# A convolution by minimal filtering: two outputs per four products, or four outputs per six

## The chip, the cores and the metric

The program runs on one core of a Trainium2 chip. Time is the device time of one launch in microseconds (us), from three runs; the profile is of one execution. The engines are named as the profile names them: PE (TensorE, matrix products; PEld its weight loads), DVE (VectorE), ACT (ScalarE), POOL (GpSimd) and SP (SyncE, which here only issues DMAs). Each engine runs its own list of instructions in order, and semaphores hold it where it needs another's result.

## The reference

Two blocks follow each other on x, of 2 batches x 1024 positions x 1024 channels, float32:

```
x = x + attention(layernorm(x))
    conv: 3 taps along the positions, 1024 -> 768 channels, padding 'SAME', + bias
    split into q, k, v of 256; 16 heads of 64, in blocks of 128 positions
    causal softmax(q k / 8) v; output 1024 -> 256, projection 256 -> 1024
x = x + lora_dense(layernorm(x))
    x W^T + b, plus four small expert products weighted by a softmax router
```

All is float32. The change is in the convolution: y[t] = w0 x[t-1] + w1 x[t] + w2 x[t+1], where each w is a 1024 x 768 matrix, and in the order in which positions lie in memory behind it.

## The kernel before, in words

**Stages.** The layer norm of a batch goes tile by tile (128 positions): DVE makes statistics, POOL the power, ACT or DVE scales, PE transposes eight 128x128 pieces, and ACT copies them from PSUM to `xT`, where channels lie on partitions. Then comes the convolution, then attention in steps of two heads and 256 positions, then the dense part in 16 tiles of 128 positions.

**The products.** The convolution takes pairs of positions. For every pair, each of the 8 chunks of 128 input channels and each of 6 chunks of 128 output channels, four products are summed over chunks in four PSUM banks: of differences and sums of four neighbouring inputs (`u`, by DVE in `transform`) with w0, w2, and (w0 + w2 +- w1)/2 (made by POOL's three additions in `mix`; the half comes at the evacuation). A "step" is one chunk of output channels of one batch, 12 in all; it has 512 pairs, so each product has 512 columns, and there are 8 chunks x 4 = 32 products in a step.

**Native and split.** Three steps multiply float32 as it is (`native_unit`). The other nine use `three_pass`: both operands are split in a high part, rounded by ACT to the short type fp32r (`high_weight`, `high_input`), and a low part, the rest, by DVE (`low_weight`, `low_input`), and PE runs high x high, high x low and low x high:

```
    pe.matmul(out, w_hi, x_hi, start=first, stop=False)
    pe.matmul(out, w_hi, x_lo, start=False, stop=False)
    return pe.matmul(out, w_lo, x_hi, start=False, stop=last)
```

**Order.** It is written out by hand. `ORDER` lists 48 slots (k) of two input chunks each; tables (`U_AT`, `HIGH_AT`, `LOW_AT`, `TURN_AT`, `STATS_AT`) say in which slot each engine does what for the second batch beside the products of the first. Raw weights are loaded by SP in a ring of `RR` = 3, split weights lie in a ring of `WR` = 2: the high part for slot k + 1 waits until PE has left slot k - 1. At the end of a step ACT evacuates one bank with the bias and DVE adds the others (`outputs`), and SP stores the result `cy` in DRAM (`c_scratch`), from where attention loads it by groups of 256 positions (`c_raw`); ACT and POOL split it again (`c_hi`, `c_lo`).

**Hand-over to attention.** The load of group 0 is issued in slot 31 and that of group 1 in slot NK - 2. Queries and keys of attention steps 0 and 1 are computed inside the last two slots of the convolution. The last step's outputs are made by DVE behind attention step 2, for `HEAD` = 3.

## Time and profile before

| | us |
|---|---|
| three runs | 915.65, 916.17, 920.49 |
| median | 916.17 |
| span of the profiled execution, first to last instruction | 915.3 |
| PE busy | 873.6 |
| DVE, ACT, POOL busy | 439.7, 395.7, 326.3 |

The profiled execution's own time on the device isn't listed apart from the three runs; its span lies 0.9 us under their median and 0.4 us under the lowest, which is what lies around a span. Matmuls are pipelined and their ends are modelled: their starts tell the pace. A wait is listed under the engine that ended it.

### The profile page before, as it was taken

The page shows a single profiled execution, that of the slowest core. Times are in us where ns is not written, and L with a number is a line of the kernel's source. Part 1 is how long each engine was busy: PE and PEld are TensorE (multiplying, and loading weights), DVE is VectorE, ACT ScalarE, POOL GpSimd, SP SyncE. Part 2 cuts the span into 40 slices and gives each one's busy share as a digit, 9 for nine tenths or more (in the row PEclk, how much of TensorE's full clock was granted, in tenths as well). Part 3 has the DMA queues.
Part 4 walks back from the last instruction along what each step waited for, and adds up shares of the span by engine and source line. Part 5 has one row for each costly group of instructions (what it writes and reads, how often), then busy time and mean ns, then how long its engine had stood idle before and what let it go on. Part 6 is the DMA issues. An engine that isn't in the chain of part 4 may idle for free.

```text
span 915.3 us, 14506 instructions
## 1 busy us (share of the span) xinstructions
PE 873.6 (95%) x5376; PEld 726.6 (79%) x5376; DVE 439.7 (48%) x1238; ACT 395.7 (43%) x1024; POOL 326.3 (36%) x295
## 2 busy tenths in 40 slices
PE   3799999998999979999999999999988999999997
PEld 3345788846888868888888888888867999999997
DVE  6944774958453333433323332433267444444442
ACT  5601332741332256867676767676674111111110
POOL 3454756548665222433343424342223100000000
PEclk9899999999999999999999999999999999999999
DMA  6145333225433332012125232020312312221211
GB/s 235 41 137 182 94 92 95 74 72 187 131 104 94 121 116 105 1 35 93 35 93 218 94 88 98 31 93 1 139 61 79 116 52 87 93 92 50 90 47 47
DMA packets 41291, 85.01 MB, mean 93 GB/s; under 512 B 9091, under 2 KB 27523, under 8 KB 40580
## 3 DMA queue, kind: packets, MB, share of 16 engines
q1 hardware_dynamic: 38916, 75.69, 25.2%
q0 software_dynamic: 2304, 8.39, 2.2%
q8 instruction: 43, 0.70, 0.3%
q14 instruction: 28, 0.23, 0.1%
HBM read 60.60 MB, written 23.07 MB: 91 GB/s over the span
## 4 chain that ended last, share of the span: by engine, by line
PE 88%; DVE 5%; ACT 2%; issue 2%; DMA 1%; POOL 1%; DVEq 0%; ACTq 0%
PE net_psum L62 20%; PE net_psum L63 19%; PE net_psum L64 19%; PE net_psum L913 8%; PE net_psum L997 4%; PE net_psum L1036 4%; PE net_psum L1004 4%; PE net_psum L1051 3%; PE net_psum L1052 2%; PE net_psum L1053 2%; PE net_psum L1065 2%; PE net_psum L895 1%; DVE x_lo L661 1%; PE net_psum L1121 1%; PE net_psum L906 1%
## 5 line engine op out<-in xcount | busy, mean ns | idle before, releaser
L405 POOL TENSOR_TENSOR pr<-pr,rrec 128x512 f32<-128x512 f32 x64 | 66.6, 1041 | 244.7 <-DVE rrec L708 244.7
L62 PE MATMUL net_psum<-fw_hi,xT_hi 128*128 128x354 f32 (+1 forms) x384 | 126.5, 329 | 0.0
L64 PE MATMUL net_psum<-fw_hi,xT_lo 128*128 128x354 f32 (+1 forms) x384 | 124.9, 325 | 0.0
L63 PE MATMUL net_psum<-fw_lo,xT_hi 128*128 128x354 f32 (+1 forms) x384 | 124.8, 325 | 0.0
L62 PE MATMUL net_psum<-x_hi,w_hi 128*128 128x512 f32 x288 | 114.3, 397 | 4.1 <-DVE w_lo L666 4.1
L63 PE MATMUL net_psum<-x_lo,w_hi 128*128 128x512 f32 x288 | 112.8, 392 | 0.0
L64 PE MATMUL net_psum<-x_hi,w_lo 128*128 128x512 f32 x288 | 112.7, 391 | 0.0
L715 DVE CUSTOM_DVE_ANT_0 pr<-net_psum,mask 128x128 f32<-128x128 f32 x256 | 58.8, 286 | 103.3 <-PE net_psum L997 103.3
L522 ACT ACTIVATE pr<-pr,negmax 128x128 f32<-128x128 f32 x256 | 99.0, 390 | 12.5 <-DVE negmax L715 12.5
L473 ACT ACTIVATE w_hi<-raw 128x1024 fp32r<-128x1024 f32 x36 | 38.1, 1058 | 134.9 <-PE net_psum L64 88.8
L385 POOL TENSOR_TENSOR raw<-raw 128x256 f32<-128x256 f32 x48 | 56.5, 1177 | 95.8 <-DMA raw<-in_conv_w 95.8
L913 PE MATMUL net_psum<-u,raw 128*128 128x512 f32 x192 | 85.6, 608 | 4.8 <-DVE u L650 4.8
L666 DVE TENSOR_TENSOR w_lo<-raw,w_hi 128x1024 fp32r<-128x1024 f32 x36 | 50.5, 1402 | 80.2 <-ACT w_hi L473 80.1
L62 PE MATMUL net_psum<-c_hi,wqk_hi 128*128 128x256 f32 x256 | 78.6, 307 | 2.6 <-ACT kf L529 2.6
L913 PEld LDWEIGHTS net_psum<-u,raw 128*128 128x128 f32 x192 | 37.3, 195 | 51.3 <-issue 50.7
L64 PE MATMUL net_psum<-c_hi,wqk_lo 128*128 128x256 f32 x256 | 73.3, 286 | 0.0
L63 PE MATMUL net_psum<-c_lo,wqk_hi 128*128 128x256 f32 x256 | 73.2, 286 | 0.0
L63 PEld LDWEIGHTS net_psum<-fw_lo,xT_hi 128*128 128x128 f32 x384 | 72.9, 190 | 0.0
L64 PEld LDWEIGHTS net_psum<-fw_hi,xT_lo 128*128 128x128 f32 x384 | 72.9, 190 | 0.0
L62 PEld LDWEIGHTS net_psum<-fw_hi,xT_hi 128*128 128x128 f32 x384 | 72.7, 189 | 0.0
L62 PEld LDWEIGHTS net_psum<-x_hi,w_hi 128*128 128x128 f32 x288 | 54.4, 189 | 16.9 <-DVE w_lo L666 5.2
L438 POOL DMA_DIRECT2D out<-y x16 | 9.4, 585 | 156.3 <-DVE y L804 156.3
(137 smaller groups left out, 1892.6 us busy)
## 6 DMA issues: line engine op xcount, KB each, us to landing
raw<-in_conv_w SPq DMA_DIRECT2D x48, 384.0 KB, 3.7
xn<-in_x SPq DMA_DIRECT2D x16, 512.0 KB, 5.0
xr<-in_x SPq DMA_DIRECT2D x8, 1024.0 KB, 4.9
x_scratch<-xr SPq DMA_DIRECT2D x8, 1024.0 KB, 4.0
x1t<-x_scratch SPq DMA_DIRECT2D x16, 512.0 KB, 4.1
out<-y POOLq DMA_DIRECT2D x16, 512.0 KB, 5.0
c_scratch<-cy SPq DMA_DIRECT2D x12, 512.0 KB, 3.3
c_raw<-c_scratch SPq DMA_DIRECT2D x8, 768.0 KB, 4.8
```

The source lines that it names most:

```text
L62: pe.matmul(out, w_hi, x_hi, start=first, stop=False)
L63: pe.matmul(out, w_hi, x_lo, start=False, stop=False)
L64: return pe.matmul(out, w_lo, x_hi, start=False, stop=last)
L385: pool.tensor_tensor(r[:, :, 3], r[:, :, 1], r[:, :, 2], ALU.add).then_inc(s["sum_ready"], 1)
L405: pool.tensor_tensor(pr[:, jj % 4], pr[:, jj % 4], rrec[:, jj % 4].unsqueeze(2).to_broadcast([P, UN, P]), ALU.mult).then_inc(s["p_ready"], 1)
L473: act.activation(w_hi[:, r % WR], raw[:, k % RR, :, 1:5], ACT.Copy).then_inc(s["w_hi_ready"], 1)
L522: e = act.activation(pr[:, jj % 4, un], pr[:, jj % 4, un], ACT.Exp, bias=negmax[:, jj % 2, un:un + 1], scale=-1.0, accum_out=rsum[:, jj % ...
L666: dve.tensor_tensor(w_lo[:, r % WR], raw[:, k % RR, :, 1:5], w_hi[:, r % WR], ALU.subtract).then_inc(s["w_lo_ready"], 1)
L715: m = dve.tensor_tensor_reduce(out=pr[:, jj % 4, un], in0=scp[:, h, b * P:(b + 1) * P], in1=mask[:], scale=-DH ** -0.5, scalar=-MASKED, op ...
L913: mm = pe.matmul(acc[st % 2][:, v, :], raw[:, k % RR, c % 2, 1 + v], u[:, c, v], start=c == 0, stop=c == DC - 1)
L997: mm = pe.matmul(scp[:, h, t], qf[e, jj % 2, t], kf[e, jj % 2, t], start=True, stop=True)
L1004: mm = pe.transpose(ptp[:, un * P:(un + 1) * P], pr[:, jj % 4, un], ident[:])
```

## The change

The pairs become quads: four outputs from six products. Every point has 256 quads a batch (`QUADS`), 512 over both (`QT`).

- Two of the six products, those with the raw taps w0 and w2, are native float32, `first_unit`, for all 6 output chunks: 24 units `a`, each two input chunks x two output chunks x two points, of 256 columns, one batch after the other. Their inputs `ua` are made by DVE (`first_inputs`), two operations of 512 elements for a chunk of a batch. ACT takes the sums to `stage`, SP stores them in DRAM (`m_scratch`) and loads them again for the outputs.
- The other four products are split passes of 512 columns over both batches, `split_unit`: 24 units `k`, each two input chunks of one output chunk. Their inputs `u` take DVE six operations per chunk and batch (`inputs_of`, 256 to 512 elements) or seven to eight for both batches (`inputs`), then one high part and one low part of 2048 elements per chunk. Their weights are taps scaled by ACT (`pre_scale`), one sum of 512 elements by POOL and two by DVE (`mix`).
- Both batches are normalised and transposed before the split units; the second one's transposes stand behind units 4 to 7. The evacuation writes four planes of positions apart (`stepped`), so all tokens lie within a tile in the order residue by residue of 4. Loads of x, stores of the result and the causal mask follow that order: each such DMA becomes two of 64 rows (four where it had two tiles), the mask four operations.
- The outputs take two ACT operations and ten of DVE in three groups (`halves`, `sums`, `ends`) per output chunk of both batches, where a step of one batch took one and four.
- Attention steps 0 and 1 stand behind the convolution. The loads of group 0 and of the attention biases are issued in slot NK - 2, behind the store of the fifth output; output chunk 5 of group 0 is taken from SBUF. The load of group 1 stands behind the store of the last output.

The core of the diff:

```diff
+    DUOS = MC // 2
+    NP4 = DC // 2
+    NA = N * DUOS * NP4
+    NK = MC * NP4
+    AW, RR, WR, ST = 4, 3, 2, 4
...
             def conv_slot(k):
-                if k in LOAD_AT:
...
+                if k == NK - 2:
+                    sync.wait_ge(s["unit_done"], k)
+                    sync.dma_start(wv_raw[:], wv).then_inc(s["wv_loaded"], 16)
+                    sync.wait_ge(s["c_stored"], 16 * LAST)
+                    sync.dma_start(c_raw[:, 0:LAST], c_dram[0:LAST, :, 0:GT].rearrange("m p l -> p m l")).then_inc(s["early_loaded"], 16)
                     for dst, src in ((bqk_c[:, 0], bq), (bqk_c[:, 1], bk), (bv_c[:], bv), (bo_c[:], bo)):
                         sync.dma_start(dst, src).then_inc(s["early_loaded"], 16)
...
-                    sync.wait_ge(s["c0_lo_ready"], 1)
-                    load_c(1)
...
+            load_c(1)
...
-                pool.wait_ge(raw_loaded[k % RR], 16 * (k // RR + 1))
-                pool.tensor_tensor(r[:, :, 3], r[:, :, 1], r[:, :, 2], ALU.add).then_inc(s["sum_ready"], 1)
-                pool.wait_ge(s["sum_ready"], k + 1)
-                pool.tensor_tensor(r[:, :, 4], r[:, :, 3], r[:, :, 0], ALU.subtract)
-                pool.tensor_tensor(r[:, :, 3], r[:, :, 3], r[:, :, 0], ALU.add).then_inc(s["mix_ready"], 1)
+                pool.wait_ge(s["pre_ready"], k + 1)
+                pool.tensor_tensor(r[:, :, 3:5], r[:, :, 1:3], r[:, :, 3:5], ALU.add).then_inc(s["ef_ready"], 1)
 
...
+            def pre_scale(k):
+                r = raw[:, k % RR]
+                act.wait_ge(raw_loaded[k % RR], 32 * (k // RR + 1))
+                act.activation(r[:, :, 2], r[:, :, 1], ACT.Copy, scale=0.5)
+                act.activation(r[:, :, 4], r[:, :, 3], ACT.Copy, scale=2.0).then_inc(s["pre_ready"], 1)
...
+            def first_inputs(n, c):
+
+                cols = slice(n * QUADS, (n + 1) * QUADS)
+                for i in range(c, c + 2):
+                    dve.scalar_tensor_tensor(ua[:, i, :, cols], pair(i, n, P2, P1), -5.0, pair(i, n, P0 + 1, P3), ALU.mult, ALU.add).then_inc(s["ua_part"], 1)
+                for i in range(c, c + 2):
+                    dve.wait_ge(s["ua_part"], DC * n + i + 1)
+                    dve.scalar_tensor_tensor(ua[:, i, :, cols], pair(i, n, P0, P3 - 1), 4.0, ua[:, i, :, cols], ALU.mult, ALU.add).then_inc(s["ua_ready"], 1)
...
+            def mix(k):
+
+                r = raw[:, k % RR]
+                tap = r[:, :, 0:1].to_broadcast([P, 2, 2, P])
+                dve.wait_ge(s["ef_ready"], k + 1)
+                dve.tensor_tensor(r[:, :, 1:3], r[:, :, 3:5], tap, ALU.add)
+                dve.tensor_tensor(r[:, :, 3:5], r[:, :, 3:5], tap, ALU.subtract).then_inc(s["mix_ready"], 1)
...
+                a, o = acc[m % 2], cy[m]
+                b2, b4 = (a[:, v].rearrange("p (b i) -> p b i", i=32) for v in (M2, M4))
+                dve.wait_ge(s["t_ready"], 2 * m + 1)
+                dve.scalar_tensor_tensor(o[:, :, O0], b2, C_A, o[:, :, O1], ALU.mult, ALU.add)
+                dve.scalar_tensor_tensor(o[:, :, O1], b2, -C_A, o[:, :, O1], ALU.mult, ALU.add)
+                dve.wait_ge(s["t_ready"], 2 * m + 2)
+                dve.scalar_tensor_tensor(o[:, :, O2], b4, C_B, o[:, :, O3], ALU.mult, ALU.add)
+                dve.scalar_tensor_tensor(o[:, :, O3], b4, -C_B, o[:, :, O3], ALU.mult, ALU.add).then_inc(s["halved"], 1)
+
...
+                o = cy[m][:, lo:hi]
+                m5, m0 = (ma[m][:, v].rearrange("p (b i) -> p b i", i=32)[:, lo:hi] for v in range(2))
+                dve.wait_ge(s["halved"], m + 1)
+                dve.wait_ge(s["ma_loaded"], 16 * (m + 1))
+                dve.scalar_tensor_tensor(m0, m0, 0.25, o[:, :, O2], ALU.mult, ALU.add)
+                dve.tensor_tensor(m5, m5, o[:, :, O1], ALU.add)
+                dve.scalar_tensor_tensor(o[:, :, O2], o[:, :, O2], 4.0, o[:, :, O0], ALU.mult, ALU.add)
+                return dve.scalar_tensor_tensor(o[:, :, O1], o[:, :, O3], 2.0, o[:, :, O1], ALU.mult, ALU.add)
...
+                m5, m0 = (ma[m][:, v].rearrange("p (b i) -> p b i", i=32)[:, lo:hi] for v in range(2))
+                dve.tensor_tensor(o[:, :, O0], o[:, :, O0], m0, ALU.add)
+                return dve.scalar_tensor_tensor(o[:, :, O3], o[:, :, O3], 8.0, m5, ALU.mult, ALU.add)
...
-                        dve.tensor_tensor(wqk_lo[:, i], wqk_raw[:, i], wqk_hi[:, i], ALU.subtract).then_inc(s["qk_w_lo_ready"], 1)
+                if k == 0:
+                    low_input(DC - 1)
+                if k + 2 < NK:
+                    mix(k + 2)
+                if m >= 0 and k % NP4 == 0:
+                    halves(m)
+                if m >= 0 and k % NP4 == 1:
+                    sums(m, 0, TOK // P).then_inc(s["add_step"], 1)
+                    dve.wait_ge(s["add_step"], m + 1)
+                    ends(m, 0, TOK // P).then_inc(s["cy_ready"], 1)
...
+            for c in range(0, DC, 2):
+                first_inputs(1, c)
+            for c in range(DC):
+                if c == DC - 2:
+                    mix(0)
+                    mix(1)
+                inputs(c)
+                if c:
+                    low_input(c - 1)
+                if c == DC - 2:
+                    low_weight(0)
+            for k in range(NK):
                 conv_slot(k)
...
+            sums(LAST, 0, GB).then_inc(s["add_done"], 1)
+            dve.wait_ge(s["add_done"], 1)
+            ends(LAST, 0, GB).then_inc(s["head_ready"], 1)
+            dve.wait_ge(s["c5_hi_ready"], 1)
...
+            sums(LAST, GB, TOK // P).then_inc(s["add_done"], 1)
+            dve.wait_ge(s["add_done"], 2)
+            ends(LAST, GB, TOK // P).then_inc(s["cy_ready"], 1)
...
+            def first_unit(a):
+
+                n, p, d = a // (DUOS * NP4), a % NP4, a // NP4
...
+                for c in range(2 * p, 2 * p + 2):
+                    pe.wait_ge(s["ua_ready"], DC * n + c + 1)
+                    for mi in range(2):
+                        for v in range(2):
+                            mm = pe.matmul(duo_acc(d, mi)[:, v * QUADS:(v + 1) * QUADS], wa[:, a % AW, mi, c % 2, 1 - v],
+                                           ua[:, c, v, n * QUADS:(n + 1) * QUADS], start=c == 0 and v == 0, stop=c == DC - 1,
+                                           skip_group_check=True)
+                mm.then_inc(s["a_done"], 1)
...
+            def split_unit(k):
+
+                m, p = k // NP4, k % NP4
+                pe.wait_ge(s["w_lo_ready"], k + 1)
+                if p == 0:
...
+                for c in range(2 * p, 2 * p + 2):
+                    if m == 0:
+                        pe.wait_ge(s["x_lo_ready"], c + 1)
+                    for v in range(NV):
+                        mm = three_pass(pe, acc[m % 2][:, v, :], w_hi[:, k % WR, c % 2, v], w_lo[:, k % WR, c % 2, v],
+                                        x_hi[:, c, v], x_lo[:, c, v], c == 0, c == DC - 1)
                 mm.then_inc(s["unit_done"], 1)
-
...
+            for a in range(NA):
+                first_unit(a)
+                for j in TURN_AT.get(a, ()):
+                    transpose_tile(1, j)
             for k in range(NK):
-                conv_slot(k)
...
```

## Rows read from the trace of the kernel before

**Rows 1.** the page, busy time by engine; chain that ended last.
```profile
PE 873.6 (95%) x5376; PEld 726.6 (79%) x5376; DVE 439.7 (48%) x1238; ACT 395.7 (43%) x1024; POOL 326.3 (36%) x295
...
PE 88%; DVE 5%; ACT 2%; issue 2%; DMA 1%; POOL 1%; DVEq 0%; ACTq 0%
```

**Rows 2.** windows: stretch; length, busy (count) by engine, PE clock, DMA share, GB/s.
```profile
28.77:86.06 57.29, 57.29 (x129) 25.25 (x129) 35.88 (x32) 16.97 (x10) 24.84 (x21) 0.95 0.37 122
...
86.06:203.00 116.94, 115.36 (x498) 87.86 (x497) 83.21 (x111) 47.03 (x41) 69.98 (x68) 1.00 0.30 92
...
230.00:326.60 96.60, 96.60 (x438) 80.08 (x436) 40.70 (x37) 27.81 (x29) 47.83 (x47) 1.00 0.40 128
...
350.00:700.00 350.00, 345.37 (x2725) 287.51 (x2725) 133.75 (x675) 241.30 (x798) 124.05 (x90) 0.99 0.23 80
```

**Rows 3.** PE's waits: waiting line, releaser, us in total, times, longest.
```profile
PE net_psum L913 <- DVE u L650: 4.8, 1, 4.8
...
PE net_psum L62 <- DVE w_lo L666: 4.1, 2, 2.6
```

**Rows 4.** timeline of PE, three stretches: start us, us, engine, line, operation.
```profile
84.31 0.19 PEld L913 LDWEIGHTS net_psum<-u,raw 128*128 128x128 f32 x1 [0.24 <-issue]
...
84.74 0.19 PEld L913 LDWEIGHTS net_psum<-u,raw 128*128 128x128 f32 x1 [0.24 <-issue]
...
90.58 0.39 PE L62 MATMUL net_psum<-x_hi,w_hi 128*128 128x512 f32 x1
...
91.26 0.39 PE L62 MATMUL net_psum<-x_hi,w_hi 128*128 128x512 f32 x1
...
322.51 0.28 PE L63 MATMUL net_psum<-c_lo,wqk_hi 128*128 128x256 f32 x1
...
322.63 0.28 PE L64 MATMUL net_psum<-c_hi,wqk_lo 128*128 128x256 f32 x1
```

**Rows 5.** chain of waits: eight transposes in a row; start us, us, what.
```profile
721.28 0.87 PE net_psum L1065 x8
```

**Rows 6.** timeline, DVE and POOL: start us, us, engine, line, operation, tiles.
```profile
25.14 1.23 DVE L648 TENSOR_TENSOR u<-xT 128x1024 f32<-128x1024 f32 x1 [2.72 <-ACT xT L455]
...
172.06 1.23 DVE L650 TENSOR_TENSOR u<-xT 128x512 f32<-128x512 f32 x1
...
178.46 0.68 DVE L649 TENSOR_TENSOR u<-xT 128x512 f32<-128x512 f32 x1
...
179.06 0.68 DVE L650 TENSOR_TENSOR u<-xT 128x512 f32<-128x512 f32 x1
...
208.50 2.67 POOL L387 TENSOR_TENSOR raw<-raw 128x256 f32<-128x256 f32 x1
```

**Rows 7.** windows, near the start.
```profile
30.00:32.00 2.00, 2.00 (x3) 0.77 (x3) 2.00 (x4) 0.57 (x1) 0.89 (x1) 0.50 0.00 0
```

**Rows 8.** groups by form: line, operation, tiles, count | busy, mean ns | idle.
```profile
L666 DVE TENSOR_TENSOR w_lo<-raw,w_hi 128x1024 fp32r<-128x1024 f32 x36 | 50.5, 1402 | 80.2 <-ACT w_hi L473 80.1
...
L661 DVE TENSOR_TENSOR x_lo<-u,x_hi 128x2048 fp32r<-128x2048 f32 x16 | 40.3, 2551 | 12.2 <-PE net_psum L913 12.2
...
L473 ACT ACTIVATE w_hi<-raw 128x1024 fp32r<-128x1024 f32 x36 | 38.1, 1058 | 134.9 <-PE net_psum L64 88.8 <-POOL raw L388 46.2
...
L405 POOL TENSOR_TENSOR pr<-pr,rrec 128x512 f32<-128x512 f32 x64 | 66.6, 1041 | 244.7 <-DVE rrec L708 244.7
```

**Rows 9.** DMA issues: tiles, queue, count, KB each, median us to landing.
```profile
c_scratch<-cy SPq DMA_DIRECT2D x12, 512.0 KB, 3.3
...
c_raw<-c_scratch SPq DMA_DIRECT2D x8, 768.0 KB, 4.8
```

**Rows 10.** timeline at the start of attention, ACT and PE.
```profile
337.91 0.83 ACT L533 ACTIVATE c_hi<-c_raw 128x768 fp32r<-128x768 f32 x1
...
343.18 0.66 PE L1004 MATMUL net_psum<-ident,pr 128*128 128x128 f32 x4
```

**Rows 11.** tile raw: one group's duration in ns, min/median/max.
```profile
L387 POOL TENSOR_TENSOR raw<-raw x48: 724/742/7260, 21.9 to 305.2; 128x256 f32<-128x256 f32 x48
```

More of the change, by code:

```diff
@@ L109, in act_scaled @@
     def act_scaled(n, j):
-        return (LT - len(DVE_SCALES)) * n + sum(i not in DVE_SCALES for i in range(j + 1))
-    def splits(k):
-        return 0 <= k < NK and not native[k]
+        return LT + j + 1 - len(DVE_SCALES) if n else sum(i not in DVE_SCALES for i in range(j + 1))
     NG = TOK // GT
@@ L247, in network, with turned, duo_acc, pair @@
         block = ctx.enter_context(nc.Block())
-        def turned(n, i):
-            if n == 0:
-                return acc[i % 4 // 2][:, 2 * (i % 2):2 * (i % 2) + 2, :]
-            return acc[0 if i < 6 else 1][:, 2 * (i % 2):2 * (i % 2) + 2, :]
+        def turned(n, j):
+            i = 2 * (j % 4) if n == 0 else 2 * (j % 2)
+            return psum[:, i:i + 2]
+        def duo_acc(d, mi):
+            return psum[:, 4 + 2 * (d % 2) + mi]
+        def pair(c, n, first, second):
+            row = (N * c + n) * ROW
+            return stepped(xT, row + first, (second - first, 2), (1, QUADS))
+        def both(c, first, second):
+            return stepped(xT, N * c * ROW + first, (second - first, 2), (ROW, N), (1, QUADS))
         def is_step(jj):
@@ L437, in store @@
                 pool.wait_ge(s["y_ready"], NB * (t + 1))
-                pool.dma_start(out[t * P:(t + 1) * P], y[:, t % 2]).then_inc(y_stored[t % 2], 16)
+                for half in range(2):
+                    pool.dma_start(rows_by_quads(out[t * P:(t + 1) * P], half), y[64 * half:64 * half + 64, t % 2]).then_inc(y_stored[t % 2], 16)
             for t in range(TT):
@@ new lines, in first_out, with high_input @@
+            def first_out(d):
+                act.wait_ge(s["a_done"], NP4 * (d + 1))
+                for mi in range(2):
+                    i = 2 * d + mi
+                    wait(act, a_stored[i % ST], 16 * (i // ST))
+                    act.activation(stage[:, i % ST].rearrange("p v i -> p (v i)"), duo_acc(d, mi), ACT.Copy).then_inc(s["a_evac"], 1)
+            def high_input(c):
+                act.wait_ge(s["u_ready"], c + 1)
+                act.activation(x_hi[:, c], u[:, c], ACT.Copy).then_inc(s["x_hi_ready"], 1)
@@ L497, in conv_slot @@
-                if k == QK_AT:
+                if k == 0:
+                    high_input(DC - 1)
+                if k % NP4 == 0 and k:
+                    evacuate(k // NP4 - 1)
+                if k + 2 < NK:
+                    pre_scale(k + 2)
+                if k in (10, 14):
+                    i = (k - 10) // 4
                     act.wait_ge(s["qk_w_loaded"], 16 * 2)
-                    for i in range(2):
-                        act.activation(wqk_hi[:, i], wqk_raw[:, i], ACT.Copy).then_inc(s["qk_w_hi_ready"], 1)
```

521 lines of the change are left out of this document (279 added, 242 removed).

## The prediction

> **What bounds the kernel now.** First the page's busy times and the chain of work that ended last: PE is busy 873.6 of 915.3 us and holds 88% of the chain; DVE and ACT are under half busy [rows 1]. The reader is to see there that only PE time is worth anything. Second the stages: PE is full in the native stage (28.77 to 86.06), in the split stages and in attention, at full clock but for short stretches [rows 2]. Third PE's waits: in the whole convolution it waits 4.8 us at the start for the first DVE inputs and 4.1 us for low weights [rows 3]. So the convolution, 28.8 to 326.6 us, is as long as its matmul columns. Fourth PE's pace: three split passes of 512 columns start every 0.68 us, 0.2267 us each; a native 512-column matmul leaves two records, each with its weight load, 0.43 us apart; a 256-column pass starts every 0.12 us [rows 4].
>
> **PE work removed and added.** Before: 9 of 12 steps are split, 9 x 32 x 3 = 864 passes; after: 6 x 8 x 4 x 3 = 576. 288 x 0.2267 = 65.3 us go. Native before: 96 matmuls of 512 columns, 192 records. After: 6 x 8 x 2 points x 2 batches = 192 matmuls of 256 columns, 384 records. Low end: half of 0.43, 0.215 each, 82.4 us, as now. High end: 256 columns cost 0.12/0.2267 = 0.53 of 512 in split passes, so 0.228, 87.4 us. I take 0.217, 83.3 us, near the low end, since the fixed part of a native record is small. The 64 transposes of the second batch stay, 0.109 us each by my estimate from eight of them in 0.87 us [rows 5], 7.0 us.
>
> **First stage, on the clock of the trace.** DVE begins its inputs at 25.1 as now [rows 6]; twice as many x DMAs of half the rows could move this by 0 to 0.5 us, taken as 0. It needs three 512-element operations and one wait for its own result before PE can start. Clean operations of 512 start 0.60 apart [rows 6], so PE starts at 25.1 + 1.9 = 27.0 against 28.77. Later inputs come at 2.5 us a pair of chunks against 3.47 us of PE, hidden. PE's clock is 0.50 in the window from 30 us [rows 7], and that costs 2.7 us of work today; I keep it (0 to 4). ACT scales and evacuates the second batch inside units 4 to 7, about 18 us of ACT in 24; hidden. DMA: 0.5 MB per 3.47 us is 151 GB/s; the same stage now moves 122 GB/s at a share of 0.37 [rows 2], so some 330 is to be had. PE ends the stage at 27.0 + 83.3 + 7.0 + 2.7 = 120.0.
>
> **Hand-off to the split stage, where I expect DVE late.** Transposes end at 27.0 + 2.7 + 8 x 3.47 + 7.0 = 64.5, their evacuation at 66. From there DVE runs without a gap: inputs of the second batch, 16 x 0.60 + 0.4 = 10; then, by 0.07 + n/960 us per operation of n elements (which gives 0.60 for 512), a second-half input of chunks 0 to 3 is 2.8, of chunks 4 to 7, both batches, 5.05; a low input is 2.2 when POOL is still (the mean with POOL beside it is 2.55 [rows 8]). Up to the first low weight: 10 + 4 x 2.8 + 3 x 5.05 + 6 x 2.2 + 5.5 (two mixes, 1.3 each, and about 3 us behind ACT's pre-scale, which stands behind two evacuations, and POOL) + 1.2 = 56.3, done at 122.3. PE waits 2.3. Before the second low weight stand one input 5.1, a low input 2.2, and itself 1.2 (1.4 in the mean today [rows 8]): 130.8; PE was due at 127.7 and waits 3.1. The third stands behind the last low input, POOL's sum, the mix, ACT's high weight: 2.2 + 2.3 + 1.1 + 1.3 = 137.7 against 136.2, 1.5. In all 6.9 us, and 1.3 for half clock after such a gap. Behind a late low weight stands only PE; all of it is on the path. Bounds: 0, if DVE finds 10 us that I double-counted, to 16, if each of some 75 operations costs its full 0.68 rather than its 0.60 step and each wait more.
>
> Here the Trainium skill would charge more. The steps of 0.60 under durations of 0.68 [rows 6] show overlap of neighbours. The page VectorE: DVE Perf Modes, section The DRAIN you can't avoid, says that after every operation the next doesn't start until the pipe is empty; by that every operation costs its whole duration, and the sum would be 75 x 0.08 = 6 us longer (867). The row speaks against it for operations with no wait between them.
>
> **Split stage.** 24 units of 24 passes, 24 x 5.44 = 130.6 us. Per unit DVE has a mix (2 x 0.60) and a low weight (1.15); per four units also 10 operations of 512 for the outputs, 6.2: 4 x 2.4 + 6.2 + 1 of waits = 16.8 of 21.8 us. The order is tighter than the sum: high weight 1.06 (ACT), pre-scale 0.7 (two of 256, from that), POOL's sum 1.04 by its 128x512 row [rows 8], mix 1.2 and 0.4 of semaphores make a loop of 4.4 us per unit against 5.44, with evacuation 5.7 in one of four. The low weight behind the six sums then comes about 0.8 us before PE wants it. A POOL operation that meets a DVE one on SBUF adds about 0.55 to it (1.23 instead of 0.68) [rows 6]; twice that for 512 elements. So between 0 and 2 us at each of five seams; I take 0.5, 2.5 in all. PE's split work ends at T = 120.0 + 6.9 + 1.3 + 130.6 + 2.5 = 261.3. Check: 326.6 less 2.9 (queries and keys of two steps that lie inside the convolution now), less 65.3, plus 0.9 native, less 1.8 start, less 5.5 old waits and their slow clock, plus 10.7 new ones is 262.7.
>
> **Start of attention.** Two head steps that lay under the last units now come after T, and two loads are late. (1) Outputs 0 to 4 are in DRAM only after DVE's fifth outputs at T - 7: store 3.3, load of c_raw with four bias loads 4.8 [rows 9] and issues: T + 1.5; ACT's high part 1.3, DVE's low part 1.4: T + 4.3, and only then queries and keys of step 0. (2) DVE goes on: halves 2.5, sums of two blocks 1.2, waits for ACT's copy and PE's second step until 10.0, first maxima 0.9, sums of fourteen blocks 3.4: T + 14.4. Store 3.3, load 4.8: c_raw of group 1 at T + 22.7. ACT's step 3 waits for it; today the load is issued before the convolution ends and ACT splits it at 337.91, 11.3 after [rows 10]. Behind this wait on ACT stand its copy 0.8, the transposed probabilities 0.6, the exponentials 1.5, q and k 0.9; PE's step 5 waits for the last: T + 26.4. Today PE starts those queries just after the four transposes of 343.18 [rows 10], at 343.9, 17.3 after. One more us for half clock: 27.4 - 17.3 = 10.1 us given back. Bounds: 3 (both loads hidden, only the 2.9 of PE work) to 14. From there attention is PE-bound at full clock [rows 2] and its code is the same; more, smaller loads and stores of x and out are hidden, with 0.5 (0 to 1) at the last store.
>
> **Sum.** 915.3 - (326.6 - 261.3) + 10.1 + 0.5 = 860.6. The profiled span lies 0.9 under the median of 916.17 (915.65 to 920.49), so I forecast 861.5.
>
> **Rivals.** A: as above, 861.5, own range 854 to 869; chance 0.50.
> B: DVE keeps up and the two loads are hidden in PE's backlog. 861.5 less 10.7 and 5 is 846. For it: DVE is only 48% busy [rows 1]. Against it: the queue in DVE after 66 us is counted from rows and leaves no gap. 0.16.
> C: DVE is later than I think: 6 us more in the hand-off, 1.5 more at each of five seams, 2 of clock: 877. For it: POOL's 256-element operation took 0.74 in the median and up to 7.3 [rows 11]. Against it: POOL has no work while most of the inputs are made. 0.29.
> D, slower than before: the serial loop of the weights takes the place of PE. If each POOL sum waits out a DVE operation (2.7, as L387 takes beside a low input [rows 6], and 0.6 for its greater length) and each mix is doubled by it (2.4), the loop is 1.06 + 0.7 + 3.3 + 2.4 + 0.4 = 7.9 us per unit, 24 x (7.9 - 5.44) - 2.5 = 56.5 more: 918. From 7.7 us a unit on nothing is left of the gain. Against it: in this order DVE mostly waits for POOL's sum, so only the low weight is beside it. 0.04. That the split passes weren't cut can't be: the count follows from the loops. That the 256-column native records cost as much as 512 ones (943) is excluded by the 0.12 against 0.2267; 0.01 with what I forgot, inside no change.
>
> The page SBUF — State Buffer, section Who interferes with whom, says that a DVE instruction with two SBUF inputs and a GpSimd one that reads SBUF shut each other out for a whole instruction. It is the rule by which D would come about; the rows agree (1.23 against 0.68 [rows 6]), but only where both have work at once.
>
> **Numbers.** A, B, C are faster: 0.95; same 0.01; slower 0.04. About 0.5% (4.6 us) is what a measurement of this kernel can tell from no change. From 847 to 880 holds B's end, A, and most of C.
>
> **What would show it.** 576 split passes, and 384 native records near 0.217 apart. PE's first native matmul near 27, its first split one near 122, waits for low weights or x_lo of about 7 us in the first three units, and little at the seams. PE's last split pass near 261. DVE without a gap from 66 to 130. ACT's first c_hi of group 1 waiting for a DMA some 5 us, about 23 us after the last pass. A mean POOL sum over 2 us or a pace of units well over 5.44 would show C or D; no PE waits around 120 would show B. The forecast is wrong in kind if attention's pace of later steps changes at all.

## The result and the profile after

The changed kernel takes 1092.05 us, median of 4 runs (1088.8 to 1093.62), against 916.0 us of the kernel before on the same chip: a ratio of 1.190, 95% interval [1.186, 1.194]. It is 19% slower where 861.5 (847 to 880) and "faster" had been forecast. Sign and size are both wrong.

The page of the kernel after, for [rows 1]: busy time, and the chain that ended last (the profiled span is 1087.0 us).

```profile
PE 835.5 (77%) x5280; PEld 727.1 (67%) x5280; DVE 451.7 (42%) x1337; ACT 390.8 (36%) x1068; POOL 209.3 (19%) x194
...
PE 47%; SPq 15%; issue 10%; DVE 10%; DMA 8%; POOL 5%; ACT 4%; DVEq 0%; POOLq 0%; ACTq 0%
...
L63 PE MATMUL net_psum<-x_hi,w_hi 128*128 128x512 f32 x192 | 77.5, 404 | 6.7 <-DVE w_lo L804 6.5
...
xn<-in_x SPq DMA_DIRECT2D x32, 256.0 KB
xr<-in_x SPq DMA_DIRECT2D x32, 256.0 KB
```

PE does less work, as forecast: 3 x 192 = 576 split passes, 835.5 us busy against 873.6. But it holds 47% of the chain and not 88%. SP's queue, nowhere in the chain before, holds 15%, DMA 8%. What waits, in the groups of waits (line, releaser, us in total, times, longest), first PE, then DVE, then POOL:

```profile
PE net_psum L1092 <- DMA wa<-in_conv_w: 64.4, 1, 64.4
PE net_psum L1173 <- POOL pr L463: 50.5, 6, 10.7
PE net_psum L1077 <- ACT xn L510: 46.0, 3, 29.0
...
PE net_psum L63 <- DVE w_lo L804: 6.5, 5, 3.0
...
DVE cstats L734 <- DMA xn<-in_x: 132.4, 15, 13.6
...
POOL xr L472 <- DMA xr<-in_x: 133.7, 7, 28.9
```

All three large PE waits lead back to a load of x. In the first stage DVE waits for the x tiles themselves; the native weights wa stand in SP's queue behind the x tiles of the second batch and come 64.4 us late; in attention, POOL waits for xr, the rows of x to be added, and its normalizations of probabilities, for which PE waits, stand behind that. Against the few us of waits of [rows 3] this is another kernel. What the loads do, by SP's part of the timeline, by tile xn (duration in ns, min/median/max) and by windows (length, busy by engine, PE clock, DMA share, GB/s):

```profile
27.47 34.90 SPq L290 DMA_DIRECT2D xn<-in_x  x6
...
L290 SPq DMA_DIRECT2D xn<-in_x x32: 504/4848/10297, 2.0 to 152.1; - x32
...
20.00:40.00 20.00, 2.88 (x12) 2.48 (x13) 3.43 (x10) 3.40 (x3) 1.10 (x2) 1.00 0.13 52
203.48:244.96 41.48, 41.48 (x193) 36.51 (x193) 39.60 (x59) 13.51 (x14) 0.00 (x0) 1.00 0.65 199
580.00:600.00 20.00, 12.30 (x84) 10.36 (x84) 3.99 (x22) 7.84 (x27) 8.43 (x5) 0.74 0.21 70
```

The DMA engines are busy at a share of 0.13, two of sixteen, and move 52 GB/s; nothing else is under way. In the median, one DMA of 256 KB keeps SP for 4.85 us before the next can be issued. The kernel before loads the same x from 4 to 10 us at a share of 1.01 and 402 GB/s:

```profile
4.00:10.00 6.00, 0.00 (x0) 0.00 (x0) 4.15 (x11) 0.82 (x1) 1.12 (x2) 1.00 1.01 402
```

The second of the changed kernel's three windows is a native stretch without transposes: 192 records (193 in the window) in 41.46 us, 0.216 each, for a forecast of 0.217. The third is attention at a place where xr is late: PE 12.3 of 20 us busy, and the clock at 0.74, a mean between its two levels, behind the idle time.

### The profile page after: what moved, and what is told of

The parts are those of the page before. It is cut to its first block, busy times and chain, and to the rows that moved or that the text cites. A ratio compares the mean times of both kernels' runs of the same rounds, so it can differ in the third digit from the quotient of the medians.

```text
span 1087.0 us, 14438 instructions
## 1 busy us (share of the span) xinstructions
PE 835.5 (77%) x5280; PEld 727.1 (67%) x5280; DVE 451.7 (42%) x1337; ACT 390.8 (36%) x1068; POOL 209.3 (19%) x194
## 4 chain that ended last, share of the span: by engine, by line
PE 47%; SPq 15%; issue 10%; DVE 10%; DMA 8%; POOL 5%; ACT 4%; DVEq 0%; POOLq 0%; ACTq 0%
SPq L290 12%; PE net_psum L63 10%; PE net_psum L64 9%; PE net_psum L65 9%; PE net_psum L1092 5%; DMA xr<-in_x 4%; PE net_psum L1173 3%; SPq L296 2%; PE net_psum L1166 2%; PE net_psum L1205 2%; POOL raw L446 2%; DVE raw L797 2%; POOL xr L472 2%; PE net_psum L1220 1%; DMA wa<-in_conv_w 1%
## 5 line engine op out<-in xcount | busy, mean ns | idle before, releaser
L1092 PE MATMUL net_psum<-ua,wa 128*128 128x256 f32 x384 | 88.5, 394 | 67.6 <-DMA wa<-in_conv_w 64.4
L1092 PEld LDWEIGHTS net_psum<-ua,wa 128*128 128x128 f32 x384 | 75.6, 198 | 79.3 <-DMA wa<-in_conv_w 64.8
L1173 PE MATMUL net_psum<-ident,pr 128*128 128x128 f32 x256 | 44.6, 300 | 53.6 <-POOL pr L463 50.5
L1077 PE MATMUL net_psum<-ident,xn 128*128 128x128 f32 x128 | 23.0, 349 | 80.9 <-ACT xn L510 46.0
L63 PE MATMUL net_psum<-x_hi,w_hi 128*128 128x512 f32 x192 | 77.5, 404 | 6.7 <-DVE w_lo L804 6.5
L64 PE MATMUL net_psum<-x_lo,w_hi 128*128 128x512 f32 x192 | 76.4, 398 | 0.0
L65 PE MATMUL net_psum<-x_hi,w_lo 128*128 128x512 f32 x192 | 76.4, 398 | 0.0
L1077 PEld LDWEIGHTS net_psum<-ident,xn 128*128 128x128 f32 x128 | 19.9, 183 | 83.6 <-ACT xn L510 37.5
L886 DVE TENSOR_TENSOR xr<-net_psum,xr 128x512 f32<-128x512 f32 x32 | 22.0, 690 | 124.9 <-PE net_psum L65 114.2
L592 ACT ACTIVATE pT<-net_psum 128x512 f32<-128x512 f32 x64 | 38.2, 598 | 95.0 <-PE net_psum L1173 94.7
```

The source lines that it names most:

```text
L592: act.activation(pT[:, jj % 2].rearrange("p b t -> p (b t)"), ptp, ACT.Copy).then_inc(s["pT_ready"], 1)
L886: dve.tensor_tensor(xr[:, k, cols], vy[n % 2], xr[:, k, cols], ALU.add).then_inc(s["x1_ready"], 1)
L1077: t = pe.transpose(turned(n, j)[:, c // 4, (c % 4) * P:(c % 4 + 1) * P], xn[:, n, j, c * P:(c + 1) * P], ident[:])
L1092: mm = pe.matmul(duo_acc(d, mi)[:, v * QUADS:(v + 1) * QUADS], wa[:, a % AW, mi, c % 2, 1 - v], ua[:, c, v, n * QUADS:(n + 1) * QUADS], st ...
L1173: mm = pe.transpose(ptp[:, un * P:(un + 1) * P], pr[:, jj % 4, un], ident[:])
```

## The experiments

The two loads of x and the output store go through `rows_by_quads`, 64 rows in the order of the quads: `rearrange("(i a b) d -> b a i d", a=2, b=2)[half]`, whose outermost dimension is a = 2. Theory S: a DMA is spread over the engines by its outermost dimension. The rivals were that rows taken apart from each other are slow as such (R), and that halves of 64 partitions are (H).

**e4_outer**, the kernel before, with only the order changed in which the rows of batch 0's tiles are named. The amount of work is the same, but the rows of a tile land on other partitions, so the output is not the reference's:

```
-  sync.dma_start(xn[:, j], x[n, j * P:(j + 1) * P, :])
+  a = (128, 2, 4, 8, 16, 32, 64, 128)[j] if n == 0 else 128
+  if a < 128: rows = rows.rearrange("(p a) d -> a p d", a=a)
+  sync.dma_start(xn[:, j], rows)
```

> The kernel before the change, with the first batch's x tiles 1 to 6 loaded with other views of their rows: tile j's 128 rows are walked as a x (128/a) rows with a = 2, 4, 8, 16, 32, 64, so the rows land on other partitions (the first batch's positions are permuted within a tile; the amount of work is the same). Theory S (a DMA is spread over the 16 engines by its outermost dimension only, so an outermost 2 uses two engines, at the 52 GB/s of the changed kernel): tile 1 takes some 9.7 us, tile 2 4.9, tile 3 2.4, tiles 4 to 6 about 1.3 each, and the kernel ends 8 to 12 us later. Rival R (rows that are not neighbours in DRAM are slow): all of tiles 1 to 6 take about 9.7 us, 50 us later. Rival H (a DMA on 64 of the 128 partitions is slow): no tile is slow, since all fill 128 partitions; no change.

Measured: 939.5 us (one run, before 918.95 in the median). DVE's first statistics of the tiles, which start when a tile is there (the timeline; tiles 0, 1, 2, 3 and 4), and three windows:

```profile
5.56 0.69 DVE L635 BATCH_NORM_STATS2 cstats<-xn 128x6 f32<-128x512 f32 x1 [3.43 <-DMA xn<-in_x]
...
22.43 0.69 DVE L635 BATCH_NORM_STATS2 cstats<-xn 128x6 f32<-128x512 f32 x1 [15.15 <-DMA xn<-in_x]
...
30.36 0.69 DVE L635 BATCH_NORM_STATS2 cstats<-xn 128x6 f32<-128x512 f32 x1 [6.14 <-DMA xn<-in_x]
...
33.49 0.69 DVE L635 BATCH_NORM_STATS2 cstats<-xn 128x6 f32<-128x512 f32 x1 [1.35 <-DMA xn<-in_x]
...
35.85 0.69 DVE L635 BATCH_NORM_STATS2 cstats<-xn 128x6 f32<-128x512 f32 x1
...
6.00:10.00 4.00, 0.00 (x0) 0.00 (x0) 1.21 (x4) 0.00 (x0) 0.56 (x1) 1.00 0.37 112
10.00:14.00 4.00, 0.00 (x0) 0.00 (x0) 0.00 (x0) 0.00 (x0) 0.00 (x0) 1.00 0.96 154
...
18.00:22.00 4.00, 0.00 (x0) 0.00 (x0) 0.00 (x0) 0.00 (x0) 0.00 (x0) 1.00 1.01 217
```

DVE is idle 15.15 us for the tile with outermost 2, then 6.14 for 4, 1.35 for 8, and no more for 16: the order S gives, and not R's. The sizes missed: the tile with 2 was expected after 9.7 us, and the kernel ended 20.5 us later where 8 to 12 were expected. S was priced for one tile at a time, but SP had issued all eight tiles by 17.5 us, and the engines are busy at 0.96 from 10 us on, so the narrow tiles may have shared their engines with the wide ones behind them; no run separates this. One thing S doesn't give: with all engines busy (1.01) only 217 GB/s flow, half of 402.

**e1_xn32, e3_both32, e5_all32**: the changed kernel with DMAs of 32 rows (outermost dimension 32, twice as many DMAs), first for the x tiles only, then for xr too, then for the output as well:

```
-  for half in range(2):
-      sync.dma_start(xn[64 * half:64 * half + 64, n, j], rows_by_quads(..., half))
+  for k in range(4):   # rows.rearrange("(i a b) d -> b a i d", a=2, b=2)[k // 2, k % 2]
+      sync.dma_start(xn[32 * k:32 * k + 32, n, j], rows_by_32(..., k))
```

> The changed kernel, with each x tile of the layer norm loaded by four DMAs of 32 rows instead of two whose outermost dimension is 2 (2 x 32 rows); same rows to the same partitions. Theory S: outermost 32, so 16 engines; the loads run at some 400 GB/s again, the first native product starts near 27 us instead of 179.6, and the kernel takes about 150 us less, some 940; attention still stalls on its x loads. Rival H (few partitions are slow): 32 partitions are no better than 64, no gain, 1090 or more. Rival R (rows apart in DRAM): no gain.

> As the run before, and attention's x loads too as DMAs of 32 rows. Theory S: PE's 50.5 us of waits for the normalised probabilities in attention, which stand behind POOL's wait for these loads, go too: some 868, that is the forecast of 861.5 plus 6.7 us of a slow last store. Rival: the stalls in attention come from the other order of work; then it stays near the run before.

> As the run before, and the stores of the result as four DMAs of 32 rows from POOL's queue. Theory S: the last store lands as soon as before the change, 5 to 7 us less, some 861 to 863. Rival: the time goes into POOL's issuing (0.66 us each, four a tile), then no gain or 1 us lost.

| kernel | us, median | ratio to before, interval |
|---|---|---|
| changed kernel | 1092.05 | 1.190 [1.186, 1.194] |
| e1_xn32 | 960.51 | 1.045 [1.043, 1.048] |
| e3_both32 | 884.88 | 0.963 [0.961, 0.965] |
| e5_all32 | 881.19 | 0.959 [0.957, 0.960] |

So the x tiles cost 131.5 us, xr 75.6 and the output 3.7: 210.9 in all. These three edits alone turn a kernel 19% slower into one 4.1% faster. The changed kernel was measured on another chip than the three; there the kernel before took 916.0 us and here 918.95, a difference of up to 3 us that lies in the 131.5 too. Each of the three ended 17 to 20 us above its expectation (940, 868, 861 to 863): the forecast of 861.5 was still wrong by 19.7. The output's edit was to bring 5 to 7 us and brought 3.7, and the trace shows what is left. POOL's issue of the last stores, in the kernel before (span 915.3) and in e5_all32 (span 882.6):

```profile
910.24 0.53 POOL L438 DMA_DIRECT2D out<-y  x1 [11.65 <-DVE y L804]
```
```profile
872.64 1.93 POOL L502 DMA_DIRECT2D out<-y  x4 [10.24 <-DVE y L961]
```

From there to the end of the span it is 5.1 us before and 10.0 in e5_all32 (7.3 in f2_two64 below, 11.6 in the changed kernel). So the four stores of 32 rows still cost 4.9 us more at the end than one of 128, and most of that is not the transfer. The trace has POOL's last instruction but for semaphores, a drain behind its wait for the stores: POOL is past that wait 2.9 us after the issue before and 4.2 in e5_all32, and the drain then takes 1.4 and 5.3 us. In f2_two64, with two stores a tile, it takes 2.7; in the changed kernel, behind a store of 11.0 us, 0.2.

**f2_two64** separates the outermost dimension from the size and number of the DMAs: two DMAs of 64 rows per tile as in the changed kernel, each with its rows in one stride.

```
-  return rows.rearrange("(i a b) d -> b a i d", a=2, b=2)[half]
+  return rows.rearrange("(i b) d -> b i d", b=2)[half]
```

> The changed kernel with the same number of DMAs, of rows in each and of bytes for x, for x again in attention and for the output (two of 64 rows per tile), but each names its 64 rows in one plain stride of two rows, so that the outermost dimension is 64 and not 2. What is left out: the order of the rows within a half is another one, so the output is not the reference's; the work is the same. Theory S (a DMA is spread over the engines by its outermost dimension): about 881, as with DMAs of 32 rows; the x DMAs leave SP about 0.5 us apart and the stretch from 10 to 20 us has a DMA share of 0.8 or more. Rival H (two DMAs of 64 partitions each are what is slow, whatever the order in which the rows are named): 1092 as the changed kernel, 4.85 us from one x DMA to the next, DMA share 0.13. Rival C (half the number of DMAs is what separates it from the version with 32 rows each, apart from any spreading): some number between, 930 to 1000.

Measured: 879.97 us (878.2 to 880.71), ratio 0.958 [0.956, 0.960]. As S says (881); H (1092) and C (930 to 1000) are out. From 10 to 20 us:

```profile
10.00:20.00 10.00, 6.44 (x31) 5.62 (x32) 8.33 (x24) 6.63 (x7) 2.79 (x5) 1.00 1.04 236
```

The half rate is here too, with 64 rows to a DMA and with every second row (8 KB) as with every fourth. What makes it isn't settled; it comes with rows that don't follow each other.

**f1_natural**: the tiles contiguous as before; the order by quads is made where ACT takes the transposed tile out of PSUM.

```
-  sync.dma_start(xn[32 * k:32 * k + 32, n, j], rows_by_32(..., k))     # four of them
+  sync.dma_start(xn[:, n, j], x[n, j * P:(j + 1) * P, :])
-  turned(n, j).rearrange("p b (c k t) -> p (b c) k t", k=4, t=32)
+  turned(n, j).rearrange("p b (c t k) -> p (b c) k t", k=4, t=32)
```

> The changed kernel with DMAs of 32 rows for x in attention and for the output, but each x tile of the convolution comes in one contiguous DMA of 128 rows, as in the kernel before, and the order by quads is made where the transposed tile leaves PSUM (ScalarE reads every fourth column; the order of the four planes in xT is changed to fit). Against the version with DMAs of 32 rows everywhere (881.2). Theory (the strided tiles arrive 2.25 us apart at 201 to 267 GB/s and that, not VectorE's 1.7 us a tile, delays the first stage: its first native matmul started at 31.9 against 27.0 forecast): tiles back at VectorE's pace, native start at 27 to 28, and 4 to 5 us less, 876.5 (875.5 to 878). Rival 1 (stage one is held up elsewhere, by ScalarE's scaling of a tile 1.24 plus evacuation 1.03 = 2.27 us a tile, which happens to be the same pace): native start stays at 31 or later, 880 to 881.5. Rival 2 (the strided read of PSUM doubles the 1.03 us of an evacuation): slower, 881 to 890.

Measured: 876.12 us (873.38 to 876.16), ratio 0.953 [0.951, 0.956], 5.1 less. The first native matmul and the first split pass of this kernel, and the first native one of e5_all32, in PE's timeline:

```profile
27.30 12.88 PE L1096 MATMUL net_psum<-ua,wa 128*128 128x256 f32 x52 [3.27 <-DVE ua L759]
...
121.87 0.50 PE L63 MATMUL net_psum<-x_hi,w_hi 128*128 128x512 f32 x1 [3.04 <-DVE w_lo L808]
```
```profile
31.94 8.35 PE L1097 MATMUL net_psum<-ua,wa 128*128 128x256 f32 x30 [3.22 <-DVE ua L760]
```

The theory's 876.5 is met and both rivals are out: native starts at 27.3, and ACT's copy out of PSUM takes as long as before (1.037 us for 1.034). With the loads as fast as before, the forecast's own times hold: 27.0 and 122.3 were forecast.

**f3_sums**: e5_all32 with the sums of the last output step's other 448 columns ahead of the first attention steps on DVE.

```
             ends(LAST, 0, GB).then_inc(s["head_ready"], 1)
+            sums(LAST, GB, TOK // P).then_inc(s["add_done"], 1)
+            dve.wait_ge(s["add_done"], 2)
+            ends(LAST, GB, TOK // P).then_inc(s["cy_ready"], 1)
             dve.wait_ge(s["c5_hi_ready"], 1)
             ...
             for J in range(HEAD): attention_step(0, J)
-            (the same three lines)
```

> The version with DMAs of 32 rows everywhere (881.2), with one change: VectorE makes the sums of the last output step's other 448 columns (six operations, 3.9 us) straight behind those of the first 64, while it waits for ScalarE's split of that head (it stood idle for 4.7 us there), and not after the first three attention steps. Theory (attention's start is held by the last store of the convolution: store issued at 289.25, its data back as c_raw at 297.9, queries of step 5 at 301.5, 32.2 us after the convolution's last product against 17.3 before the change): the store goes out at about 283.5, c_raw is there at 292, step 5's queries start at 295.7 to 296.5, and 5 to 5.8 us are saved: 875.8 (875 to 877.5). Rival (attention is paced by its own chain through VectorE and ScalarE over the first group, and the group's 12 steps give it back; or the clock stays low longer): 879.5 to 881.5.

Measured: 871.92 us (870.7 to 873.43), ratio 0.950 [0.948, 0.952], 9.3 less and not 5.8. The stores and loads of c and ACT's split of group 1, then three windows after the last split pass, in e5_all32:

```profile
289.25 0.33 SPq L319 DMA_DIRECT2D c_scratch<-cyz  x1
293.14 0.38 SPq L322 DMA_DIRECT2D c_raw<-c_scratch  x1
...
297.86 0.84 ACT L614 ACTIVATE c_hi<-c_raw 128x768 fp32r<-128x768 f32 x1 [5.33 <-DMA c_raw<-c_scratch]
...
289.30:299.30 10.00, 5.72 (x45) 4.47 (x44) 1.82 (x18) 3.81 (x13) 2.60 (x3) 0.94 0.50 184
299.30:309.30 10.00, 8.90 (x49) 8.22 (x50) 1.18 (x10) 8.46 (x26) 4.78 (x4) 0.67 0.01 2
309.30:319.30 10.00, 10.00 (x68) 8.59 (x68) 4.42 (x20) 4.43 (x15) 1.39 (x2) 0.71 0.83 234
```

and in f3_sums:

```profile
283.02 0.33 SPq L319 DMA_DIRECT2D c_scratch<-cyz  x1
286.91 0.38 SPq L322 DMA_DIRECT2D c_raw<-c_scratch  x1
...
291.59 0.85 ACT L614 ACTIVATE c_hi<-c_raw 128x768 fp32r<-128x768 f32 x1 [0.89 <-DMA c_raw<-c_scratch]
...
289.00:299.00 10.00, 9.83 (x76) 8.39 (x74) 2.11 (x18) 9.11 (x27) 3.93 (x3) 1.00 0.20 69
299.00:309.00 10.00, 10.00 (x79) 8.68 (x78) 3.87 (x14) 6.74 (x25) 3.85 (x3) 0.83 0.43 146
309.00:319.00 10.00, 10.00 (x89) 8.43 (x86) 3.06 (x21) 7.01 (x25) 2.08 (x2) 1.00 0.42 93
```

The store goes out 6.2 us earlier, as expected. What it brought beyond that goes with the clock. In e5_all32 PE is idle for 4.3 of 10 us and then works 20 us at a mean clock of 0.67 and 0.71, a loss of 3.3 + 2.9 by my estimate from these rows; with no such gap it loses 1.7. The difference, 4.5, covers the 3.5 that the expectation lacked; f3_sums loses a little of it before, with a clock of 0.66 against 0.74 in the first 20 us, where PE is busy for half the time in both. Both figures are of one execution each, and that of e5_all32 was the slowest of its four: the two spans differ by 12.7 us, the medians by 9.3.

**f4_best** has both edits and a third: bias loads early, c0 split ahead of wv on ACT and DVE.

```
+  (slot 4)   bias loads, out of slot NK - 2
   (ACT)      - high_values(); c0_hi          + c0_hi; high_values()
   (DVE)      - wv_lo; c_lo of c0; halves     + c_lo of c0; wv_lo; halves
```

> Both of the two edits (contiguous x tiles; the last sums first), and in addition the four bias loads go out with wq and wk early in the split stage, and ScalarE and VectorE split c0 ahead of wv, since the first query matmul waited 7.3 us for c0's low part and that stood behind the split of wv (c_lo 275.0, wv_lo 271.9 to 274.2). If the terms add up: 881.2 - 4.7 - 5.4 - 1 = 870 (868.5 to 872.5). If the start of attention has one limit only, so that the earlier QK(0) brings nothing: 871 to 872. If rivals hold (native start unchanged, attention self-paced): 878 to 881.

Measured: 869.05 us (867.56 to 872.47), ratio 0.948 [0.945, 0.950], as the terms add up (870).

**g1_two** is f1 and f3 together and nothing else. **g2_handoff** adds one move on DVE:

```
-                if c == DC - 2: mix(0); mix(1)
                 inputs(c)
+                if c == DC - 2: mix(0); mix(1)
```

**g3_start** adds another order at the start of attention:

```
   (slot 4)   + bias loads, out of slot NK - 2
   (ACT)      - high_values(); c0_hi; evacuate(LAST)
              + evacuate(LAST); c0_hi; high_values()
   (DVE)      - wv_lo; c_lo of c0; halves, head sums; other sums
              + halves, head sums; c_lo of c0; other sums; wv_lo
```

> The version with DMAs of 32 rows for x in attention and for the output, with both single edits: each x tile of the convolution in one contiguous DMA (alone 881.2 to 876.1, native start 31.9 to 27.3) and the convolution's last sums ahead of the first attention steps (alone 881.2 to 871.9). If the two add up, as they sit in different stages: 881.2 - 5.1 - 9.3 = 866.8 (865.5 to 868.5). Then the third edit of the version that measured 869.1 (bias loads early, c0 split ahead of wv, wv's low part ahead of the last sums) cost 2 us, by the store of the last output step 2 us later on VectorE. If they do not add up, and that edit is neutral: 869 to 870.

> The previous one with one change at the hand-off: VectorE mixes the first two weights after the seventh chunk's inputs and not before them. In the version with contiguous x tiles it stood idle 2.9 us there for GpSimd's mix, and TensorE then waited 3.0 us for the first low weights (first split matmul 121.9, native ended 118.9) and 0.9 and 1.1 at the next two, with the clock at half for 2.6 us behind the first gap. Theory (these waits are VectorE's order and nothing else): the low weights are there at about 118.5, when the native stage ends; first split at 118.9 to 119.5, the second unit waits under 1 us, the clock does not fall: 3.5 to 4.5 us less, 862.8 (861.5 to 864). Rival (VectorE is short of time in all of 66 to 130, so that what it gains here it gives back at the next units): 865 to 867.

> The previous one with another order at the start of attention: ScalarE evacuates the last convolution step at once, while it waits for c0 (it stood idle there 13.7 us), splits c0 next and wv last; VectorE makes the last step's outputs (first 64 columns), splits c0, makes the other sums, and makes wv's low part last; the four bias loads go out with wq and wk. Theory (attention's start is still set by when the last output step is stored): store 9 to 11 us after the last split product (14.5 in the version with the sums first), c_raw of group 1 there before ScalarE asks for it (it waited 0.9 to 2.3 us for it), 2 to 4 us less, 860 (858.5 to 862). Rival (what limits it by now is the softmax chain of the first five steps on VectorE and ScalarE, with TensorE's clock low): within 1 us of the previous one.

| kernel | us, median (range) | ratio to before, interval |
|---|---|---|
| g1_two | 868.94 (865.97 to 871.31) | 0.946 [0.943, 0.948] |
| g2_handoff | 863.97 (862.19 to 866.45) | 0.943 [0.940, 0.945] |
| g3_start | 865.25 (861.97 to 866.46) | 0.941 [0.939, 0.944] |

g1_two lies at f4_best's time, within both ranges: the third edit of f4 is worth nothing that can be told. The two single gains, 5.1 and 9.3, come to 12.3 together and not to 14.4. g2_handoff's median is 5.0 lower, inside the range that its theory gave (861.5 to 864), though the intervals overlap a little; the trace says otherwise. The first three units of the split stage in PE's timeline, in g1_two and then in g2_handoff:

```profile
122.83 0.51 PE L63 MATMUL net_psum<-x_hi,w_hi 128*128 128x512 f32 x1 [3.02 <-DVE w_lo L808]
131.16 0.50 PE L63 MATMUL net_psum<-x_hi,w_hi 128*128 128x512 f32 x1 [0.92 <-DVE w_lo L808]
138.01 0.50 PE L63 MATMUL net_psum<-x_hi,w_hi 128*128 128x512 f32 x1 [0.98 <-DVE w_lo L808]
```
```profile
118.46 0.50 PE L63 MATMUL net_psum<-x_hi,w_hi 128*128 128x512 f32 x1 [1.01 <-DVE w_lo L808]
126.80 0.50 PE L63 MATMUL net_psum<-x_hi,w_hi 128*128 128x512 f32 x1 [2.49 <-DVE w_lo L808]
133.64 0.51 PE L63 MATMUL net_psum<-x_hi,w_hi 128*128 128x512 f32 x1 [1.00 <-DVE w_lo L808]
```

Little of the theory holds. The first low weights are there 2 us earlier after native's end, but the second unit now waits 2.49 for 0.92: the waits sum to 4.5 against 4.9, so DVE, short of time here, took it back, as the rival said. In these two profiles the third unit starts 4.4 us earlier. Of that, 0.7 is an earlier native start (27.34 for 28.00) and 1.6 a clock of 1.00 and not 0.73 from 26 to 32 us, where the two kernels are the same, so neither is the edit's; 0.4 is the waits, and 1.7 the clock behind the shorter gap (1.00, against 0.67 and 0.90 in two windows of four us). That is some 2 us for the edit; its medians say 5.0 with intervals that overlap, and what lies between stays open. The two profiles are g1_two's slowest execution and g2_handoff's fastest: their spans differ by 9.1, and 4.7 of it lie behind the last split pass, where the two kernels are the same. In g3_start the store of c goes out at 271.4, 2.2 earlier than in g2_handoff and 10.4 behind the last split pass, ACT no longer waits for c_raw, and the time is the same: what limits the start of attention by then is not that load. That it is the softmax chain, as the rival has it, isn't shown. PE's first query still waits 7.2 us for c0's low part (7.4 in g2_handoff), because c0 arrives no earlier for being asked first: its load takes 6.4 us from its issue.

## Why the prediction was wrong, point by point

**The step that failed** is in "First stage": "twice as many x DMAs of half the rows could move this by 0 to 0.5 us, taken as 0", and its twin in "Start of attention": "more, smaller loads and stores of x and out are hidden, with 0.5 (0 to 1) at the last store". I counted DMAs and bytes and didn't read the order of the rows. The three DMA edits were booked at 0.5 us; they measure 131.5, 75.6 and 3.7, and even with 32 rows to a DMA the last store ends 4.9 us later than before. None of the rivals had this mechanism, and the range had no bound for it: the diff named access patterns that no row of the trace before showed, so "hidden" needed a bound from both sides there. At one engine's pace of 402/16 = 25 GB/s, two engines give 50 GB/s, and the 8.4 MB of the x tiles take 168 us: that bound would have been a rival with a price.

The Trainium skill states the rule, and I hadn't weighed it: DMA: Bandwidth & Descriptors, section "Why a DMA increments its semaphore by 16 and not by 1", says that a DMA runs on the largest number of engines, at most 16, that divides the outermost dimension (of size above 1) of both its sides. The trace agrees: 0.13 is 2/16 at an outermost 2, and DVE's wait shrank at 4 and 8 and was gone at 16.

**What then was right.** With the loads spread, the forecast's times within the span can be checked against e5_all32 (span 882.6, in an execution 3.1 us above its median) and f1_natural (span 874.3, in its median execution); the forecast's span was 860.6:

| step | forecast | e5_all32 | f1_natural |
|---|---|---|---|
| first native matmul | 27.0 | 31.9 | 27.3 |
| native records apart | 0.217 | 0.216 (changed kernel) | |
| split passes apart, at full clock | 0.2267 | 0.2333 | 0.2333 |
| first split pass | 122.3 | 128.1 | 121.9 |
| last split pass ends (T) | 261.3 | 269.3 | 263.1 |
| T to the end of the span | 599.3 | 613.3 | 611.2 |
| issue of the last store to the end of the span | 5.6 (5.1 before) | 10.0 | 9.9 |

- First stage: right but for the loads. The strided rows' half rate, which starts native 4.9 us late in e5_all32, was not seen.
- Hand-off: right in cause, and in size partly by offsets. Between 66 and 130 in f1_natural, DVE is idle for long only once, 2.9 us for POOL's mix. The first split pass waits 3.0 for the low weights (2.3 forecast), the second unit 0.9 and the third 1.0 (3.1 and 1.5 forecast): 5.0 in all and not 6.9. The first low weights are there 0.4 us from the forecast, since DVE starts 1.3 earlier (64.7) and takes 0.8 longer; steps of 0.68 and not 0.60 would have made it some 6 us later, by the prediction's own count of 75 operations. The page of the Trainium skill cited there (VectorE: DVE Perf Modes, The DRAIN you can't avoid) adds, which I had left out, that a next operation that isn't held starts earlier; that sentence is what the rows show.
- Split stage: 141.2 us from first to last pass against 139.0. POOL's sum takes 1.54 us in the mean where 1.04 was taken, but under the 2 us that would show C or D. The pace of the passes was wrong too. Two passes of f1_natural; the second is the 21st behind the first:

```profile
257.78 0.39 PE L65 MATMUL net_psum<-x_hi,w_lo 128*128 128x512 f32 x1
...
262.68 0.40 PE L65 MATMUL net_psum<-x_hi,w_lo 128*128 128x512 f32 x1
```

  That is 0.2333 us a pass, for 0.2267 in [rows 4]. It is so in the split stage of the changed kernel, e5_all32, f1_natural and g2_handoff alike, and comes to 3.8 us over 576 passes; what makes it stays open.
- Start of attention: the mechanism was right, the size short. In e5_all32 the store of the last step goes out at T + 19.9 (T + 14.4 forecast): c0's low part is there at T + 7.2 and not T + 4.3, and ACT's copy of the last step's head at T + 15.3 and not T + 10.0. The first of these is in part c0's load, which takes 5.9 to 6.4 us in f4_best and g3_start and not 4.8, beside wv's, which takes 7.8; splitting it ahead of wv left PE's wait at 6.6 to 7.2 us (7.3). c_raw is issued at T + 23.8, and step 5 follows at T + 32.2 (26.4). ACT waits 5.3 us for c_raw, as forecast. Given back are 14.9 us at that point and not 9.1, and the clock takes 6.2 in the 20 us behind where 1 was allowed.
- Last store: 0.5 was allowed and 4.9 came, with four stores of 32 rows in place of one: 1.3 in the stores, and the rest in POOL's drain behind them, which the prediction has no term for.
- Around the span lie 1.7 to 1.8 us in every execution whose time and span are both known (876.12 and 874.3 in f1_natural), and not the 0.9 that the forecast added.

The 230.6 us between 861.5 and 1092.05 are thus 210.9 by the spread of the DMAs and 12.3 by rows apart and the late sums with their clock, in one kernel; 7.4 stay. No experiment varied them, but the traces name 4.4 at the last store, 3.8 in the pace of the passes and 0.9 around the span, less what came out shorter at the hand-off. So with only its DMAs repaired the change would have lain 19.7 us from the forecast, just outside its range. The fastest versions, g2_handoff and g3_start, are 5.8% faster than the kernel before and lie within 4 us of 861.5, but in part by luck: they have two orders mended that the forecast had counted as they were, and that makes up for the last store and the slower passes.

## What to carry to other kernels

When a diff changes how a DMA names its rows, read the outermost dimension first: with the same bytes, and even the same number of DMAs, an outermost 2 made a kernel 19% slower that is 4% faster with 32 or 64. A DMA share that sits at a round fraction of sixteen while nothing else moves, with SP's issues as far apart as the transfers are long, is the sign of it in a profile. The remedy has its price at the end of the kernel, where nothing hides it: four stores for one cost 4.9 us there. A gap of PE costs itself and, by the clock behind it, up to as much again (here 4.5 us behind 4.3 idle, 1.7 behind 3.0, each read from one pair of profiles), so work that feeds a DRAM round trip belongs ahead of work that only fills the wait.

## What the runs showed of the hardware

- A load of 256 KB whose outermost dimension is 2 ran at a DMA share of 0.13 and 52 GB/s and kept SP 4.85 us before its next issue, in the median of 32; loads of other tensors further down SP's list came as late (PE waited 64.4 us for wa). A load doesn't always hold up the next ones: in e4_outer SP had issued all eight tiles by 17.5 us, while the tile with outermost 2 was there at 22.4, and the DMA share was 0.96 from 10 to 14 us.
- Rows of 4 KB that don't follow each other move at half the rate with all engines busy: 217 to 242 GB/s at a share of 1.01 to 1.04, against 402 GB/s contiguous. This held for every second row (f2_two64) and for every fourth (e5_all32). The cause stays open.
- ACT reads PSUM with a stride of four elements as fast as contiguously: 1.037 us in the mean for 128x1024 in f1_natural, 1.034 in e5_all32.
- Split passes of 128x512 started 0.2333 us apart at a granted clock of 1.00 in the changed kernels and 0.2267 apart in the kernel before, in the same operations. The cause stays open.
- POOL's drain at the end of the program took 1.4, 2.7 and 5.3 us behind one, two and four stores a tile from POOL's queue (before, f2_two64, e5_all32), with the stores themselves done 2.9 to 4.2 us after the first issue. Whether the last tile's stores or all of them count, no run shows.
